# A fused decoder on one core: the first cross attention's step reordered, a third buffer for half of its keys and queries, and scatters of slot rows moved to the last steps

## What is computed

```python
x = x + _L0_xattn_ref(_layernorm(x, axis=-1), ctx_1024, ctx_1024, ...)   # 16 heads of 16
x = x + _L0_ffn_ref(_layernorm(x, axis=-1), ...)
# _L0_xattn_ref
scores = jnp.einsum('bhqd,bhkd->bhqk', q, k) * inv_sqrt_d
weights = jax.nn.softmax(scores, axis=-1)
out = jnp.einsum('bhqk,bhkd->bhqd', weights, v)
# _L0_ffn_ref: 32 experts in 8 groups, 4 of each token's best groups, top 4 experts, 250 rows each
shared = jax.nn.silu(xf @ sg) * (xf @ su) @ sd
xn = _l2norm(xf)
expert_scores = xn @ _l2norm(expert_centroids).T + bias
top_scores, top_idx = jax.lax.top_k(masked, K)
pos = jnp.cumsum(onehot, axis=0)[jnp.arange(N * K), flat_e] - 1
keep = pos < capacity
buf = jnp.zeros((E + 1, capacity, d), xf.dtype).at[e_s, p_s].set(xf[tok])[:E]
```

## Time and profile before

| | us |
|---|---|
| median of 3 runs | 1789.15 (1788.22 to 1790.02) |
| the profiled execution | 1794.52 |
| its span, first to last instruction | 1792.5 |
| TensorE busy in the span | 1497.2 |
| VectorE, ScalarE, GpSimd busy | 799.8, 687.3, 461.1 |
| mean granted TensorE clock | 0.927 |

### The profile page before, as it was taken

The page is one execution under the profiler, slowest core; times in us unless marked ns, Lnnn a source line. Parts: engine busy times, 40 slices in busy tenths (PEclk is TensorE's granted clock), DMA queues, the critical chain, the costliest instruction groups (busy, mean ns, idle before and its releaser), DMA issues. The chain is left out here.

```text
span 1792.5 us, 30479 instructions
## 1 busy us (share of the span) xinstructions
PE 1497.2 (84%) x11670; PEld 1128.7 (63%) x11670; DVE 799.8 (45%) x2278; ACT 687.3 (38%) x1423; POOL 461.1 (26%) x437
## 2 busy tenths in 40 slices
PE   3989987698888799999999936988699999819992
PEld 2556554366655566888888823655467666619991
DVE  4665562467675432222222215666556766511111
ACT  1543542565554411222222212455555555503330
POOL 0221210011233353656666420111101111040003
PEclk9999998699998899999999967899899999959996
DMA  6433422977665123778778644455566776229993
GB/s 244 131 100 120 139 85 86 166 130 125 119 107 102 48 57 85 200 201 201 189 192 205 163 109 97 97 125 124 94 128 111 118 119 113 33 92 356 346 340 90
DMA packets 255033, 254.98 MB, mean 142 GB/s; under 512 B 117532, under 2 KB 228468, under 8 KB 249396
## 3 DMA queue, kind: packets, MB, share of 16 engines
q1 hardware_dynamic: 210868, 222.04, 49.0%
q0 software_dynamic: 41152, 28.50, 8.5%
q10 hardware_dynamic: 2880, 2.62, 0.4%
HBM read 195.67 MB, written 57.20 MB: 141 GB/s over the span
## 5 line engine op out<-in xcount | busy, mean ns | idle before, releaser
L2637 PE MATMUL cross_ps_score<-cross_q,cross_k 128*128 128x250 f32 x1024 | 223.5, 376 | 0.8 <-DVE cross_q L3052 0.8
L2637 PEld LDWEIGHTS cross_ps_score<-cross_q,cross_k 128*128 128x128 f32 x1024 | 195.6, 191 | 23.9 <-DVE cross_q L3052 1.0
L3061 DVE TENSOR_TENSOR cross_prob<-cross_act_,cross_ps_score 128x250 f32<-128x250 f32 x128 | 53.2, 416 | 268.3 <-ACT cross_act_ L2757 263.8
L3140 POOL DMA_INDIRECT x_sum<-cross_ye,cross_token x64 | 128.6, 2009 | 80.8 <-ACT cross_ye L2763 68.7
L1656 ACT ACTIVATE layer_parts<-layer_ps_prob 128x400 f32<-128x400 f32 (+1 forms) x192 | 96.9, 508 | 102.7 <-PE layer_ps_prob L1479 100.9
L2784 DVE TENSOR_REDUCE cross_nmax<-cross_ps_score 100x2 f32<-100x722 f32 x128 | 112.2, 904 | 48.7 <-PE cross_ps_score L2404 45.1
L2667 ACT ACTIVATE cross_prob<-cross_ps_prob 128x400 f32<-128x400 f32 (+1 forms) x192 | 94.7, 505 | 76.1 <-PE cross_ps_prob L2438 72.3
L2649 PE MATMUL cross_ps_prob<-cross_val,cross_prob 128*125 128x256 f32 x512 | 115.8, 379 | 0.0
L2757 ACT ACTIVATE cross_act_<-cross_ps_score 128x250 f32<-128x250 f32 x128 | 48.5, 379 | 167.6 <-PE cross_ps_score L2637 166.2
L2649 PEld LDWEIGHTS cross_ps_prob<-cross_val,cross_prob 128*125 128x125 f32 x512 | 93.5, 188 | 12.8
L3130 POOL DMA_INDIRECT cross_xe<-ln_rows,cross_token x64 | 79.7, 1245 | 81.8 <-PE cross_ps_misc L2623 57.6
(11 more groups left out here) (397 smaller groups left out, 2945.9 us busy)
## 6 DMA issues: line engine op xcount, KB each, us to landing
experts_w<-in_w SPq DMA_DIRECT2D x40, 1024.0 KB, 7.1
k_stack<-mixer_part SPq DMA_DIRECT2D x32, 541.5 KB, 3.5
cross_k<-in_wg SPq DMA_DIRECT2D x32, 512.0 KB
cross_k<-in_wu SPq DMA_DIRECT2D x32, 512.0 KB
cross_val<-in_wd SPq DMA_DIRECT2D x32, 512.0 KB
cross_k<-k_stack SPq DMA_DIRECT2D x32, 270.8 KB
layer_stacks<-k_stack SPq DMA_DIRECT2D x32, 270.8 KB, 5.1
mixer_ctx<-in_ctx_t POOLq DMA_DIRECT2D x16, 361.0 KB, 4.1
```

The costliest lines, as they stand in the source:

```text
L2637: ins = nc.tensor.matmul(ps_pre[m][:, side, 0:CAP], w[s][:, k, m * P:(m + 1) * P], xt[s][:, k, :], start=(k == 0), stop=(k == KD - 1))
L3140: g.indirect_dma_start(prog.x_sum, bass.IndirectOffsetOnAxis(token[:, 2 * e + t:2 * e + t + 1], 0), ye[s][:, t, :], None, compute_op=ALU.a ...
```

## The change

- The order within a step. The score units of the next step move up to places 0 and 2 to 8. One transpose `shift_rows(b + 1)` at place 11 serves both halves; its result lies in bank 3 of `ps_score`, and ScalarE copies half 0 at place 11 and half 1 at place 0 of the next step. The value products go tile by tile at places 9, 10 and 11; ScalarE copies two of them at places 10 and 11 and the third at place 0 of the next step. `turn_normal` stands at place 11, its copy behind the first exp of the next step; logits and positions follow at place 2 behind the last weigh; all these and `scaled` use `ps_misc` now. `to_rows` waits for `scaled` and, in one step of four, for `v_pos`.
- `squares` and `scaled` move from VectorE to ScalarE (Square with an accumulated sum, and Copy with a scale). One split of the maxima for all heads replaces two.
- Half 1 of keys and queries has a third buffer, in memory that the shared expert uses behind the loop. Its load for step b+2 stands at the start of step b. A fifth set of constant rows is copied ahead of the loop.
- The blank fills move from ahead of the loop to step five (b = 4).
- No scatters in steps 8 to 13. Group 0's sixteen columns go in steps 14 and 15, eight in each; groups 1 to 3, 48 columns, behind the loop.
- Expert weights for buffer 0 are loaded after the last prob unit instead of a step earlier.

```diff
--- before.py
+++ after.py
@@ -2157,14 +2157,16 @@
     NQ = H // G
     NPU = NQ * NKT
     NC_ = E0 + NGRP
+    BLANKS_AT = G
     Q_WIDE = -(-((HH - 1) * T + P) // 32) * 32
     K_WIDE = -(-((HH - 1) * S2 + NKT * P) // 32) * 32
 
-    SCORE_AT = {1: 0, 2: 1, 4: 2, 5: 3, 6: 4, 8: 5, 9: 6, 10: 7}
+    SCORE_AT = {0: 0, 2: 1, 3: 2, 4: 3, 5: 4, 6: 5, 7: 6, 8: 7}
     AV_AT = {4: 0, 7: 1, 10: 2}
-    LAST_AV, SHIFT_B, ROWS, TURN, OUT, SHIFT_A = 1, 2, 3, 5, 7, 9
-    STATS, NORMAL, LOGITS, SOFTEN = 8, 11, 1, 8
-    ROUTE_AT = (0, 2, 4, 6, 8, 10, 12, 14, 16, 20, 23, 25, 27, 29, 31, 33)
+    LAST_AV, SHIFT_B, SCALED, ROWS, TURN, OUT, SHIFT = 1, 0, 3, 4, 6, 8, 11
+    STATS, NORMAL, SQUARES, TURN_NORMAL, LOGITS, SOFTEN = 9, 10, 11, 11, 2, 8
+    VALUES_AT = {9: 0, 10: 1, 11: 2}
+    ROUTE_AT = (0, 2, 4, 6, 8, 10, 12, 14, 16, 20, 23, 25, 27, 28, 30, 32)
     HOT_PART, POS_PART = 8, 10
 
...
+        third_k = prog.act2.rearrange("p u t -> p (u t)").bitcast(BF16)[:, 0:K_WIDE]
+        third_q = prog.up2[:].rearrange("p u t -> p (u t)").bitcast(BF16)[:, 0:Q_WIDE]
+
+        def ring_of(b, h):
+
+            return b % (2 + h)
+
+        def queries_of(b, h):
+            return third_q if ring_of(b, h) == 2 else q_sb[ring_of(b, h)][:, h]
+
+        def keys_of(b, h):
+            return third_k if ring_of(b, h) == 2 else k_sb[ring_of(b, h)][:, h]
+
         ps_score = psum("ps_score", [P, 4, 512])
...
                         sp.wait_ge(pe_val, NKT * (b + 1))
                         load_src(b + 2)
                         sp.wait_ge(g_base, b + 1)
                         load_x(b + 2)
                         sp.wait_ge(pe_prob, NPU * b + NPU // 2)
                         load_half(b + 2, 0)
+                    if b == BLANKS_AT:
+                        sp.wait_ge(zero_set, 1)
+                        sp.dma_start(prog.row_token[0:SLOTS0].rearrange("(p n) o -> p (n o)", p=T),
+                                     blank[:].rearrange("p n o -> p (n o)")).then_inc(zeroed, 16)
+                        sp.wait_ge(blank_set, 1)
+                        sp.dma_start(prog.ln_rows[N:N + CAP].rearrange("(t p) d -> p t d", p=HALF), xe[0][:]).then_inc(blank_rows, 16)
+                        sp.dma_start(prog.x_sum[N:N + CAP].rearrange("(t p) d -> p t d", p=HALF), xe[0][:]).then_inc(blank_sums, 16)
                     if b > 0:
                         store_rows(b - 1)
-                    if b + 2 < B:
-                        sp.wait_ge(pe_prob, NPU * (b + 1))
-                        load_half(b + 2, 1)
                 def load_up(e):
                     for k, (dst, name) in enumerate(((wg, "wg"), (wu, "wu"))):
                         sp.dma_start(dst[e % 2], prog.ins[name][e]).then_inc(w_in[k][e % 2], 16)
@@ -2365,7 +2380,7 @@
                 def load_down(e):
                     sp.dma_start(wd[e % 2], prog.ins["wd"][e]).then_inc(w_in[2][e % 2], 16)
 
-                sp.wait_ge(pe_prob, NPU * (B - 1))
+                sp.wait_ge(pe_prob, NPU * B)
                 load_up(0)
...
-                    s, h2 = b % 2, u * 2 // NU
+                    h2 = u * 2 // NU
                     if u % (NU // 2) == 0:
-                        pe.wait_ge(half_in[h2][s], (16 + 16 * len(K_PARTS)) * (b // 2 + 1))
+                        pe.wait_ge(half_in[h2][ring_of(b, h2)], (16 + 16 * len(K_PARTS)) * (b // (2 + h2) + 1))
                     if u >= 2:
                         pe.wait_ge(v_max, b * NU + u - 1)
+                    elif b > 0 and u == 0:
+                        pe.wait_ge(a_val, NKT * b - 1)
                     elif b > 0:
                         pe.wait_ge(a_val, NKT * b)
+                        pe.wait_ge(a_shift, 2 * b)
...
+                        pe.wait_ge(v_max, NU * b + NU - 1)
+                    if t == 2:
+                        pe.wait_ge(v_max, NU * b + NU)
+                    for k in range(KD):
+                        ins = nc.tensor.matmul(ps_score[0:rows_, t, 0:D], src[s][:, k, at:at + rows_],
+                                               prog.w("x0_wv", KD)[:, k, :], start=(k == 0), stop=(k == KD - 1))
+                    ins.then_inc(pe_val, 1)
+
+                def shift_rows(b):
+                    pe.wait_ge(v_split, b + 1)
...
+                    if b > 0:
+                        pe.wait_ge(a_scaled, b)
+                    if counted_group(b + 1) is not None:
+                        pe.wait_ge(v_pos, counted_group(b + 1) + 1)
                     for q4 in range(NQ):
                         ins = nc.tensor.transpose(ps_misc[0:T, q4 * P:(q4 + 1) * P], acc[:, q4 * T:(q4 + 1) * T], ident)
...
+                shift_rows(0)
+                for t in range(NKT):
+                    values(0, t)
                 pe.wait_ge(v_bias, 1)
-                shift_rows(0, 0)
-                values(0)
-                pe.wait_ge(heads_set, 4)
+                pe.wait_ge(heads_set, 5)
                 for b in range(B):
                     for k in range(NPU):
                         prob_unit(b, k)
-                        if k == LOGITS and b >= 2:
-                            logits(b - 2, spare_bank)
-                            if counted_group(b) is not None:
-                                positions(counted_group(b), spare_bank)
                         if k == LAST_AV and b > 0:
                             weigh_values(b - 1, NQ - 1)
+                        if k == LOGITS and b >= 2:
+                            logits(b - 2, ps_misc)
+                            if counted_group(b) is not None:
+                                positions(counted_group(b), ps_misc)
                         if k in AV_AT:
                             weigh_values(b, AV_AT[k])
-                        if k == SHIFT_B:
-                            pe.wait_ge(a_shift[0], b + 1)
-                            shift_rows(b, 1)
                         if k == ROWS and b > 0:
-                            pe.wait_ge(a_shift[1], b + 1)
                             to_rows(b - 1)
                         if k == TURN and b > 0:
...
                             if k in SCORE_AT:
-                                if SCORE_AT[k] == 1 and b >= 2:
-                                    pe.wait_ge(v_scaled, b - 1)
-                                    if counted_group(b) is not None:
-                                        pe.wait_ge(v_pos, counted_group(b) + 1)
                                 score_unit(b + 1, SCORE_AT[k])
-                            if k == SHIFT_A:
-                                if b > 0:
-                                    pe.wait_ge(v_out, b)
-                                else:
-                                    pe.wait_ge(a_shift[1], 1)
-                                shift_rows(b + 1, 0)
-                    if b + 1 < B:
-                        values(b + 1)
-                    if b > 0:
-                        turn_normal(b - 1, spare_bank)
+                            if k == SHIFT:
+                                shift_rows(b + 1)
+                            if k in VALUES_AT:
+                                values(b + 1, VALUES_AT[k])
+                        if k == TURN_NORMAL and b > 0:
+                            turn_normal(b - 1, ps_misc)
 
                 last = B - 1
                 weigh_values(last, NQ - 1)
+                logits(last - 1, ps_misc)
                 shared_up(0, 0)
-                pe.wait_ge(v_out, last)
                 to_rows(last)
-                logits(last - 1, spare_bank)
                 turn(last)
-                pe.wait_ge(v_scaled, last)
                 shared_up(0, 1)
                 project(last)
...
+                for r in range(3):
+                    for h in range(r // 2, 2):
+                        nc.scalar.copy(by_head(keys_of(r, h), S2)[SHIFT_ROW:P],
                                        prog.c("head_sel")[SHIFT_ROW:P, h * HH:(h + 1) * HH].unsqueeze(2)
                                        .broadcast_to([32, HH, S2])).then_inc(heads_set, 1)
...
-                values(0)
+                for t in range(NKT - 1):
+                    values(0, t)
                 for b in range(B):
                     for k in range(NPU):
                         exp(b, k)
                         if k == SHIFT_B:
                             shift_rows(b, 1)
-                        if k == SHIFT_A and b + 1 < B:
-                            shift_rows(b + 1, 0)
+                            values(b, NKT - 1)
+                            if b >= 2:
+                                turn_normal(b - 2, ps_misc)
                         if k == LAST_AV and b > 0:
                             keep_acc(b - 1)
+                        if k == SCALED and b >= 2:
+                            scaled(b - 2, ps_misc)
                         if k == TURN and b > 0:
                             turn(b - 1)
                         if k == SOFTEN and b + 1 < B and counted_group(b + 1) is not None:
```

(48 more changed lines are left out.)

146 lines of the change are left out of this document (65 added, 81 removed).

## The result

| | us |
|---|---|
| the changed kernel, median of 4 runs | 1807.7 (1805.6 to 1809.7) |
| the kernel before beside it, median of 4 runs | 1789.6 |
| ratio | 1.010, 95% interval 1.008 to 1.013 |
| the profiled execution, its span | 1808.8, 1807.0 |

Forecast was 1776, in a range from 1757 to 1793. The kernel got slower by 18 us. Of the six comparisons that followed, the first three gave 1791 to 1792 for the kernel before again; the last three, later, gave 1770 to 1773, and there the change makes no difference.

The account below looks back on a forecast made before the run. TensorE, held in bits by the other engines, was taken to bound the loop. The terms +2.0 - 2.3 - 2.4 - 17.7 + 1.1 + 6 = -13.3 us took the median from 1789.15 to 1776, range 1757 to 1793.

Parts of the forecast that it names:

- Behind the loop: From the loop's end to the first expert: 48 scatters make the slots come later, TensorE idles 5 us more; +6 us.
- The reordered step: Plain loop steps: 14.8 us against 15.27, with gaps at the seam, logits and score unit 5; steps 1 to 4 -2.3.
- Steps 5 to 7: The three loop steps with routing: 16.3, 16.5 and 15.8, together 48.6 us against 50.99, -2.4.
- Steps 8 to 13: Six loop steps freed of their scatters: 94.5 us against 112.17, -17.7, the main term.
- The start: Prologue and first steps: value products wait for the transpose, +1.5, and loads go ahead of those needed, +0.5; +2.0 us.
- Steps 14 and 15: Last two loop steps, sixteen scatters instead of eight, root waiting behind them: +1.1 us, between -4 and +9.
- B: Rival: the hold isn't the scatters', so steps 8 to 13 keep their 12.4 us; 1788 us, chance 0.15.
- C: Rival: idle at the seam of steps lowers TensorE's granted clock to 1.2 GHz; 1798 us, chance 0.12.
- D: Rival: Square isn't in Exp's table, so each of 15 steps pays two table loads; 1811 us, chance 0.04.
- A: Rival: the seam is cheaper, TensorE near 14.1 us a step, routed steps without low clock; 1764 us, chance 0.19.
- theory P: From the experiments, not the prediction: short or dense TensorE products during a run of scatters start the hold of TensorE's signals.

Follow-up runs that it names:

- a_three_runs: The changed kernel, with GpSimd waiting behind the loop ahead of group 2's and group 3's sixteen scatters until all earlier ones landed; 1797.5 us in one run.
- after_again: The changed kernel, unchanged, run again in a later comparison where the kernel before took 1770.3 us; 1770.2 us, ratio 1.000.
- b_new_sched: The kernel before with only the new places of the scatters; 1801.6 us, ratio 1.006.
- a_none_in_loop: The changed kernel without the 32 scatters of groups 0 and 1, so none in the loop and 32 behind it; 1762.0 us in one run.
- before_again: The kernel before, unchanged, run again for its trace in a later comparison; median 1770.3 us.
- a_old_sched: The changed kernel with the old places of the scatters, four in each of steps 8 to 15 and 32 behind the loop; 1771.8 us, ratio 0.989.
- a_drained: The changed kernel, with GpSimd waiting behind the loop ahead of every further eight scatters until all earlier ones landed; 1786.6 us, ratio 0.998.
- a_quick: The changed kernel with the old scatter places, plus thirteen short unread products on TensorE within the third group's shared_up; 1781.8 us in one run.
- a_old_again: The changed kernel with the old places of the scatters, run once more; 1775.6 us, ratio 0.992.
- a_single: The changed kernel with four scatters in each of steps 8 to 15, one or two at a time, none ahead of root; 1766.7 us, ratio 0.987.
- a_drop16: The changed kernel without group 1's sixteen scatters and the waits for them; 1775.6 us, ratio 0.991.
- a_pos_late: The changed kernel with the last group's positions moved behind the third group's shared_up, with VectorE's parts behind them; 1794.6 us, ratio 1.003.

## Why the prediction was wrong

**The step that failed** is "Behind the loop", its term of +6. I had seen that scatters hold ScalarE and VectorE in the steps, and priced it at 0.5 us each there; for the tail I took that "sixteen scatters in a row hold nobody" and moved sixteen more there free of a hold. In the changed kernel the tail grew by 33.7 us; without the hold the same kernel's tail is 27.6 us shorter (85.29 against 112.85), so a hold that the term put at nothing was 27.6 of it. One observation of a quiet run was too little to price others by: a_three_runs has runs of sixteen too, and a hold. What may have kept it quiet in the kernel before is that the last group's positions fell between two runs and a whole shared_down lay only at the end of the last run; that is a guess.

**Everything else in that term was right**, as the trace without the hold shows: last scatter at +69.4 (forecast +70.1), slots issued at +71.8 (72.2), read at +74.3 (74.7), tail longer by 6.1 (6). The last is in part luck: TensorE comes to the slots' transposes 4.5 us later, not 5, and the products behind the idle lose 1.7 at a granted clock of 0.59, not 1. These three rows are of after_again:

```profile
662.16 0.99 POOL L3114 DMA_INDIRECT row_token<-cross_choice,cross_row_put  x1 [0.31 <-issue]
664.63 0.52 SPq L2396 DMA_DIRECT2D cross_slots<-row_token  x1
667.09 0.22 DVE L3055 CAST cross_slot_fields<-cross_slots 64x125 f32<-64x125 int32 x1 [2.82 <-DMA cross_slots<-row_token]
```

**The reordered step**: 14.84 measured, 14.8 forecast, and for the reasons given: score unit 5 waits 0.62 us for VectorE (0.6), the logits 0.73 for xt (1.0). Steps 5 to 7 came cheaper (14.97, 15.48, 16.50 against 16.3, 16.5, 15.8): the route parts ahead of unit 5 cost almost nothing, and the third step, where to_rows waits for v_pos, more. Steps 8 to 13: -20.6 against -17.7, the same surplus. The kernel before spent 15.8 us of its 112.17 on the scatters there (b_new_sched), not 12.4; the rest of the gain is the order's.

**The start** was mis-sized: +5.9 against +2.0. Most of it is the wait for keys in step 1. The sixteen traces that share this start have 2.0 to 5.3 us from step 1's first exp to its keep_acc, where the kernel before has 0.8, so the wait is real and its size here was near the top by chance.

**Steps 14 and 15**: step 14 took 19.68, and 19.69 without the hold, against 15.49 in a_none_in_loop; so root behind four scatters costs 4.2 (3.5 forecast) with the hold and without. Step 15 took 19.07 with the hold and 11.74 without: eight scatters in a row across the seam cost 7.3 us of hold. The change as a whole gave +4.7 in place of +1.1.

**The rivals.** B, that the hold isn't the scatters', falls: without them (a_none_in_loop, b_new_sched) it is gone from the steps. They don't suffice either (before_again). The rule weighed there, that only VectorE's and GpSimd's port pair contends and that TensorE and ScalarE never wait on anyone (the Trainium skill, "SBUF — State Buffer", section "SBUF: two separate sides"), may hold for ports, yet here ScalarE, which waits for TensorE, idles 39.82 us while GpSimd issues scatters; the measurement decides. C: the granted clock is 0.99 to 1.00 in steps 1 to 13, no dip at the seam. D: Square loads no table; a plain step is 14.84. A: its step time of 14.1 didn't come, its cheaper routed steps did. No rival put the loss behind the loop; the one that was needed was "the hold grows with what runs beside the scatters", and the earlier trace rows (2.7 us with two, 3.8 with four) already spoke of it.

**What stays open.** Shown: the hold needs scatters (a_none_in_loop, a_old_sched), pauses shorten it (a_drained), a run longer than sixteen isn't needed (a_three_runs), and in three of the seven comparisons it isn't there. Seen in one run each: thirteen short products start it (a_quick), and it begins within shared_up with neither them nor shared_down near (b_new_sched; a_old_sched, a_old_again, a_single and a_drop16 also hold one Silu there, by 1.6 to 3 us). So theory P isn't the only way in, and that 32 products of shared_down in 7.2 us start it, which would explain a_pos_late and a_drained, is argued only; the run meant to settle this met no hold. ScalarE's two table loads, which stand at 629.5 to 632.3 where the changed kernel's hold begins, were never moved by themselves; a_quick's hold begins without one. What in the chip delays TensorE or its signals wasn't found, nor why the same kernel has the hold in one comparison and not in another.

## What to carry to other kernels

Work that an engine does beside others has a price per place, not one price: if a transfer holds its neighbours in one stage, don't book it free in the next because one run of it there looked quiet; look at what each neighbour does during it. Here the small indirect transfers did at least as well spread singly over the steps as in pairs (0.987 and 0.992, with overlapping intervals), and clearly better than four or more in a row. And time a change of under 2% on more than one chip and at more than one time: here the same pair gave 1.010 and 1.000.
